# Rotary sum on another engine, output projection in token layout, first layer of a two-layer transformer on one core

## The reference

```python
q = jnp.einsum('bpd,hde->bphe', resid_pre, W_Q) + b_Q      # k, v alike
q = _apply_rotary(q, cos, sin)                             # k too: pairs (xr, xi) are turned
scores = jnp.einsum('bqhd,bkhd->bhqk', q, k) / ATTN_SCALE
scores = jnp.where(causal[None, None], scores, jnp.zeros((), dtype=scores.dtype))
max_v = jnp.max(jnp.abs(scores), axis=-1, keepdims=True)
sgn = jnp.sign(scores)
attn_w = sgn * jnp.exp(sgn * scores - max_v)
attn = attn_w / (jnp.sum(jnp.abs(attn_w), axis=-1, keepdims=True) + 1e-06)
z = jnp.einsum('bkhd,bhqk->bqhd', v, attn)
out = jnp.einsum('bqhd,hdm->bqm', z, W_O) + b_O
```

## Time and profile before

| | us |
|---|---|
| median of 3 runs | 992.29 (986.94 to 999.68) |
| the profiled execution, whole | 992.66 |
| its span between first and last instruction | 990.9 |
| first layer's heads, first to last `z_lo` | 54.4 to 452.3 |
| TensorE, VectorE, ScalarE, GpSimd busy | 866.4, 698.8, 508.4, 464.5 |

### The profile page before, as it was taken

How to read it: one execution, slowest core, us unless ns; L and a number is a source line. 1 busy time by engine, 2 the same in 40 slices (tenths; PEclk the granted TensorE clock), 3 DMA queues, 4 the chain that set the end, 5 groups by cost and what they waited for, 6 DMA issues and landing times.

```text
span 990.9 us, 14203 instructions
## 1 busy us (share of the span) xinstructions
PE 866.4 (87%) x3884; PEld 620.8 (63%) x3884; DVE 698.8 (71%) x1340; ACT 508.4 (51%) x1102; POOL 464.5 (47%) x393
## 2 busy tenths in 40 slices
PE   3799999999799999976799999578999997899997
PEld 2566666666566666654578887454444334678885
DVE  4789999989699999975755555856668814653344
ACT  2578887778578887853322222111546753222222
POOL 1646666656366666632256666422120002466663
PEclk9799999999899999997999999785789998999999
DMA  3222222222222222210033334053142100233332
GB/s 110 86 86 86 85 85 85 83 82 84 84 85 85 85 85 80 79 65 34 19 133 111 111 112 170 1 182 112 68 141 88 44 2 0 77 112 111 111 115 76
DMA packets 48270, 85.41 MB, mean 86 GB/s; under 512 B 7330, under 2 KB 18210, under 8 KB 48226
## 3 DMA queue, kind: packets, MB, share of 16 engines
q1 hardware_dynamic: 48226, 84.88, 25.3%
HBM read 58.38 MB, written 9.57 MB: 69 GB/s over the span
## 4 chain that ended last, share of the span: by engine, by line
PE 56%; DVE 18%; issue 8%; POOL 6%; ACT 6%; DMA 3%; DVEq 0%; SPq 0%; ACTq 0%; POOLq 0%
PE ps L719 16%; PE ps L731 7%; PE ps L315 5%; DVE ex L478 4%; PE ps L1236 3%; PE ps L1224 3%; DVE w L490 3%; DVE q_rot L451 3%; PE ps L366 3%; PE ps L1176 3%; PE ps L326 3%; PE ps L1155 3%; PE ps L358 2%; PE ps L348 2%; POOL q_sin L511 2%
## 5 line engine op out<-in xcount | busy, mean ns | idle before, releaser
L767 ACT ACTIVATE silu<-ps 128x512 f32<-128x512 f32 x68 | 40.7, 598 | 187.0 <-PE ps L719 187.0
L807 POOL TENSOR_TENSOR guw<-gu,cwb 128x512 f32<-128x512 f32 x64 | 96.6, 1511 | 82.9 <-DVE gu L854 65.5
L719 PE MATMUL ps<-xT_hi,ew_hi 128*128 128x512 f32 x272 | 107.6, 396 | 5.4 <-POOL ew_lo L797 5.4
L719 PE MATMUL ps<-xT_hi,ew_lo 128*128 128x512 f32 x272 | 106.2, 390 | 0.0
L719 PE MATMUL ps<-xT_lo,ew_hi 128*128 128x512 f32 x272 | 106.2, 390 | 0.0
L854 DVE TENSOR_TENSOR gu<-silu,ps 128x512 f32<-128x512 f32 x64 | 43.9, 687 | 87.7 <-PE ps L719 69.3
L797 POOL TENSOR_TENSOR ew_lo<-ew_raw,ew_hi 128x256 fp32r<-128x256 f32 (+1 forms) x68 | 80.1, 1179 | 54.4 <-DVE ew_hi L844 54.4
L1403 DVE TENSOR_REDUCE nm<-ps 128x1 f32<-128x512 f32 x128 | 81.1, 685 | 31.1 <-PE ps L1176 30.7
L451 DVE TENSOR_TENSOR q_rot<-q_cos,q_sin 128x512 f32<-128x512 f32 x64 | 86.4, 1388 | 11.5 <-POOL q_sin L511 10.1
L496 POOL TENSOR_TENSOR wqk_lo<-wqk_raw,wqk_hi 128x512 fp32r<-128x512 f32 x32 | 47.8, 1494 | 97.0 <-ACT wqk_hi L389 97.0
L490 DVE SCALAR_TENSOR_TENSOR w<-ex,rden,sgn 128x512 f32<-128x512 f32 (+3 forms) x128 | 90.7, 769 | 3.2
(11 more groups left out here) (172 smaller groups left out, 2128.5 us busy)
## 6 DMA issues: line engine op xcount, KB each, us to landing
q_sw<-q_in SPq DMA_DIRECT2D x128, 128.0 KB, 2.1
cwb<-cw_dram SPq DMA_DIRECT2D x30, 512.0 KB, 4.5
ew_raw<-in_ew SPq DMA_DIRECT2D x34, 384.0 KB, 3.0
wqk_raw<-in_wqk SPq DMA_DIRECT2D x32, 256.0 KB, 2.7
wv_raw<-in_wv SPq DMA_DIRECT2D x32, 128.0 KB, 2.3
wo_raw<-in_wo SPq DMA_DIRECT2D x32, 128.0 KB, 2.0
qs<-stk_q SPq DMA_DIRECT2D x16, 256.0 KB, 3.4
ks<-stk_k SPq DMA_DIRECT2D x16, 256.0 KB, 4.0
```

The lines of the kernel that those rows point to most:

```text
L719: last = pe.matmul(ps[:, 4 + 2 * h + u, :], ew[pw][:, p, col:col + P], half_of((xT_hi, xT_lo)[px][:, c, :], h), start=j == 0, stop=j == 3 ...
L807: pool.tensor_tensor(guw[:, h, :], gu[:, h, :], half_of(cwb[:, p, :], h), ALU.mult).then_inc(sem("guw"), 1)
```

## The change

The sum of the rotary halves moves from VectorE to GpSimd, and the sine products move there ahead of the causal masks. VectorE makes the cosine product from PSUM banks 5 and 6 with bias and cosine in one instruction, instead of from `q_in`; so TensorE now waits for `q_cos` and not for `q_ev` (the copy to `q_in`) before it writes these banks again, with the transposes and with the next projection. The output projection has `z` as its stationary and the weights as its moving operand, 12 matmuls of 256 columns instead of 6 of 512, so that the result lies in token layout as `x` does: no `aT`, no transposes back, no clearing (the first head of a batch starts the sum). The output bias of the layer, broadcast to all partitions, is added to `x` by GpSimd after steps 14 and 15. The loads of `wo`, `wv` and `wqk` have another order in SyncE's queue, and the constant rows for the second layer are written during the first experts instead of behind the last heads.

```diff
@@ a0_pe
                 for t in range(2):
+                    wait(pe, "q_cos", of_pair(n, t))
                     for j in range(3 * DC):
...
+                first = known(n) and n % H0 == 0
                 wait(pe, "z_lo", n + 1)
                 wait(pe, "wo_lo", n + 1)
-                for c in range(DC):
+                if first and n > 0:
+                    wait(pe, "x_add", 2)
+                for t in range(QT):
                     for j, (pw, pz) in enumerate(PARTS):
-                        last = pe.matmul(ps[:, c, :], wo[pw][:, c * P:(c + 1) * P], z0[pz][:, :],
-                                         start=False, stop=j == 2, skip_group_check=True)
+                        last = pe.matmul(ps[:, t // 2, t % 2 * D:(t % 2 + 1) * D], z0[pz][:, t * P:(t + 1) * P], wo[pw][:, :],
+                                         start=first and t % 2 == 0 and j == 0, stop=j == 2, skip_group_check=True)
...
                     if g:
-                        wait(pe, "q_ev", of_pair(min(n + 3, N0) if known(n) else n + 3, g - 1))
+                        wait(pe, "q_cos", of_pair(min(n + 3, N0) if known(n) else n + 3, g - 1))
@@ a0_act
                     wait(act, "q_ps", of_pair(n + 1, t))
-                    wait(act, "q_cos", of_pair(n, t))
                     wait(act, "q_sin", of_pair(n, t))
@@ a0_dve
-                    dve.tensor_tensor(q_cos[:, t, :], q_in[:, t, :], cos0[:, :], ALU.mult).then_inc(sem("q_cos"), 1)
+                    dve.scalar_tensor_tensor(out=q_cos[:, t, :], in0=ps[:, 5 + t, :], scalar=bqkv0[:, t, bass.ds(n, 1)],
+                                             in1=cos0[:, :], op0=ALU.add, op1=ALU.mult).then_inc(sem("q_cos"), 1)
...
-            if valid(i + 2, N0):
-                rotated(0)
-            if valid(i + 2, N0):
-                rotated(1)
@@ a0_pool
+                    wait(pool, "q_cos", of_pair(n + 1, t))
+                    wait(pool, "q_sin", of_pair(n + 1, t))
+                    wait(pool, "s", QT * (n - 1))
+                    pool.tensor_tensor(q_rot[:, par(2), t, :], q_cos[:, t, :], q_sin[:, t, :], ALU.add).then_inc(sem("q_rot"), 1)
@@ a0_sp
-            if valid(i + 1, N0):
-                n = i + 1
+            if valid(i, N0):
+                n = i
                 src = a["wo0"][head(n)]
                 wait(sp, "wo_lo", n)
                 sp.dma_start(wo_raw[:, :], src).then_inc(sem("wo_ld"), 16)
+            if valid(i + 2, N0):
+                n = i + 2
+                src = a["wv0"][head(n)]
+                wait(sp, "wv_lo", n)
+                sp.dma_start(wv_raw[:, :, :], src).then_inc(sem("wv_ld"), 16)
             if valid(i + 4, N0):
                 n = i + 4
                 src = a["wqk0"][head(n)]
                 wait(sp, "wqk_lo", n)
                 sp.dma_start(wqk_raw[:, :, :, :], src).then_inc(sem("wqk_ld"), 16)
...
+        def a0_at_pool(pool, i):
+            if i == H0 - 2:
+                pool.wait_ge(sem("bo0_ld"), 16)
+                pool.wait_ge(sem("xn"), NT)
+            if i in (H0 - 2, H0 - 1):
+                h = i - (H0 - 2)
+                pool.tensor_tensor(x[:, h * QT:(h + 1) * QT, :], x[:, h * QT:(h + 1) * QT, :],
+                                   bo0_b[:, :].unsqueeze(1).broadcast_to([P, QT, D]), ALU.add).then_inc(sem("x_bo0"), 1)
...
+            h = i // H0 - 1
+            dve.wait_ge(sem("x_bo0"), h + 1)
+            dve.wait_ge(sem("o"), i)
+            for k in range(2):
+                t = QT * h + 2 * k
+                dve.tensor_tensor(x[:, t:t + 2, :], x[:, t:t + 2, :],
+                                  ps[:, k, :].rearrange("p (t d) -> p t d", t=2), ALU.add).then_inc(sem("x_add"), 1)
+            if i == N0:
                 ln_stats(dve, 1, 0)
```

More of the change, by code:

```diff
@@ L184, in build_program @@
         cw_dram = [nc.dram_tensor(f"cw_dram{k}", (E, T), F32).ap() for k in range(2)]
-        bo_dram = nc.dram_tensor("bo_dram", (D,), F32).ap()
+        bo_dram = [nc.dram_tensor(f"bo_dram{k}", (D,), F32).ap() for k in range(2)]
         stk_dram = [nc.dram_tensor(f"stk_{t}", (N1 * P, S), F32).ap() for t in ("q", "k")]
@@ L445, in a0_dve @@
         def a0_dve(dve, i):
[L446 to L451, removed]
             if valid(i + 2, N0):
@@ L497, in a0_pool @@
                                    ALU.subtract).then_inc(sem("wqk_lo"), 1)
+            if valid(i + 2, N0):
+                n = i + 2
+                for t in range(2):
+                    wait(pool, f"swap{t}", 32 * (n + 1))
+                    wait(pool, "q_rot", of_pair(n, t))
+                    pool.tensor_tensor(q_sin[:, t, :], q_sw[:, t, :], sin0[:, :], ALU.mult).then_inc(sem("q_sin"), 1)
             if valid(i + 1, N0):
@@ L541, in a0_sp @@
                 sp.dma_start(wqk_raw[:, :, :, :], src).then_inc(sem("wqk_ld"), 16)
-            if valid(i + 3, N0):
-                n = i + 3
-                src = a["wv0"][head(n)]
-                wait(sp, "wv_lo", n)
-                sp.dma_start(wv_raw[:, :, :], src).then_inc(sem("wv_ld"), 16)
         batch = [0]
         odd = [0]
-        LOOPS0 = {1: (H0 - 6, 0), H0 + 1: (N0 - 6, 1)}
+        LOOPS0 = {3: (H0 - 6, 0), H0 + 3: (N0 - 6, 1)}
         def par(ahead):
@@ L567, in a0_steps @@
                     step(eng, i)
-                    if at and i in (H0, N0):
-                        at(eng, i // H0 - 1)
+                    if at:
+                        at(eng, i)
                     i += 1
-        def a0_between_sp(sp, b):
-            if b > 0:
-                return
-            ffn_sp(sp, 0)
-        def a1_early_sp(sp):
-            sp.wait_ge(sem("ones"), 1)
-            for t in range(2):
-                rows = stk_dram[t].rearrange("(b h r) s -> b h r s", b=B, r=STK)
-                for g in range(DC):
-                    for h in range(B):
-                        sp.dma_start(rows[h, g * H1 // 2:(g + 1) * H1 // 2, ROWS_S:STK, :],
-                                     fp(ones_r[:, :])).then_inc(sem("ones_st"), 16)
-            sp.dma_start(bo_dram.rearrange("(c p) -> c p", p=P), a["bo1"].rearrange("p c -> c p"), allow_slow_non_contiguous=True).then_inc(sem("bo_st"), 16)
@@ L587, in a0_zero_pe @@
-        def a0_zero_pe(pe, b):
-            if b == 0:
-                pe.wait_ge(sem("zero"), 1)
-            else:
-                pe.wait_ge(sem("x_add"), 2 * b)
-            for c in range(DC):
-                pe.matmul(ps[:, c, :], zero_r[:, 0:P], zero_r[:, :], start=True, stop=True, skip_group_check=True)
-        def a0_end_pe(pe, b):
-            back_pe(pe, "aT", 2 * b + 2, (0, 1), range(QT * b, QT * b + QT))
-            if b == 0:
-                a0_zero_pe(pe, 1)
-        def a0_end_act(act, b):
-            act.wait_ge(sem("o"), H0 * (b + 1))
-            for c in range(DC):
-                act.activation(aT[:, c, b * S:(b + 1) * S], ps[:, c, :], ACT.Identity,
-                               bias=bo0[:, c:c + 1]).then_inc(sem("aT"), 1)
@@ new lines, in ones_sp @@
+        def ones_sp(sp, t, g):
+            rows = stk_dram[t].rearrange("(b h r) s -> b h r s", b=B, r=STK)
+            sp.wait_ge(sem("ones"), 1)
+            for h in range(B):
+                sp.dma_start(rows[h, g * H1 // 2:(g + 1) * H1 // 2, ROWS_S:STK, :],
+                             fp(ones_r[:, :])).then_inc(sem("ones_st"), 16)
+        def a0_at_pool(pool, i):
[6 more added lines that the diff above has]
+                                   bo0_b[:, :].unsqueeze(1).broadcast_to([P, QT, D]), ALU.add).then_inc(sem("x_bo0"), 1)
@@ L611, in a0_end_dve, with a0_at_dve @@
+        def a0_at_dve(dve, i):
+            if i not in (H0, N0):
+                return
+            h = i // H0 - 1
+            dve.wait_ge(sem("x_bo0"), h + 1)
+            dve.wait_ge(sem("o"), i)
+            for k in range(2):
+                t = QT * h + 2 * k
+                dve.tensor_tensor(x[:, t:t + 2, :], x[:, t:t + 2, :],
+                                  ps[:, k, :].rearrange("p (t d) -> p t d", t=2), ALU.add).then_inc(sem("x_add"), 1)
+            if i == N0:
                 ln_stats(dve, 1, 0)
@@ L674, in step @@
                     load(m, p)
+                if f == 0 and known(m) and m in (2, 3, M - 3, M - 2):
+                    k = (2, 3, M - 3, M - 2).index(m)
+                    ones_sp(sp, k // 2, k % 2)
             ffn_steps(sp, step)
@@ L887, in ffn_dve @@
                 ln_xn(dve, 1, 0)
-                back_dve(dve, 2, (0, 1), range(QT, 2 * QT))
             else:
```

49 lines of the change are left out of this document (24 added, 25 removed).

## The result

The changed kernel takes 1083.55 us (median of 4 runs, 1081.76 to 1087.81) where the kernel before takes 993.52 us in the runs beside it: a ratio of 1.091, 95% interval 1.084 to 1.099. That is slower, by about 90 us; the prediction said 1105 us, with 1010 to 1135 as its range.

A forecast was written before the change was run, and what follows sets the result against it. Each first-layer head was taken as bound by a chain from transposes through VectorE's `w` to the next transposes. 992.7 + 76 (turns) + 42 (clock) - 2.5 (batch change) = 1108, stated as 1105 us, range 1010 to 1135.

The forecast's parts named there:

- Direction and mechanism: Whole kernel slower, as VectorE's `w` pieces and GpSimd operations take turns, three per head; slower beyond 2% had chance 0.80.
- Turns at `w`: First-layer heads: three GpSimd operations between the pieces of `w` instead of one, 15.3 us a head, +76 us over 28 heads.
- Cosine product from PSUM: First-layer heads: transposes wait for `q_cos`, +0.49 us a head; with -0.34 on the chain, +0.15 net.
- Rotary sum on GpSimd: First-layer heads: GpSimd's two added operations of about 1.25 us cost nothing while it has room; chain gains 0.34 us a head.
- TensorE's clock: First-layer heads: idle gaps of 3.4 us drop the granted clock to 0.50; 1.5 us a head, +42 us over 28.
- Layout: Output projection into token layout: twelve matmuls of 256 columns, 1.44 us against 1.4, so nothing.
- batch change: Between heads 16 and 17: copies, transposes and clearing go, bias additions come; net -2.5 us, between -9 and +3.
- The additions on GpSimd: Batch change: two output-bias steps of 2.37 us, each holding VectorE up once, 4.8 us.
- The end of the layer: End of the first layer: copies go, layer-norm sums stand behind the last projection; 0, between -2 and +3 us.
- the constant rows: Second layer's rows, moved into the experts' steps: cost at most their issue; 0, up to +4 us.
- the rotary part: First-layer heads: +76 us for turns, with the cosine product's part in it, and +42 us for the clock.
- the sign: Whole kernel: slower beyond 2% of 992 us, chance 0.80; within 0.08, faster 0.12.

The follow-up runs named there:

- e1: The changed kernel with GpSimd's sine product behind the causal masks again, ahead of the rotary sum: 1024.9 us, ratio 1.034.
- e2: The changed kernel with GpSimd's two sine products replaced by two memsets that read nothing from SBUF: 1018.9 us, ratio 1.031.
- e3: The changed kernel with the cosine product reading `q_in` again and the transposes waiting for ScalarE's eviction: 1075.0 us, ratio 1.084.
- e12: The kernel before with only the cosine product from PSUM, transposes and next projections waiting for it: 994.8 us, ratio 1.002.
- e11: The kernel before with masks ahead of `wqk_lo`, the changed load order, and the rotary sum on GpSimd behind the sine product: 1025.0 us, ratio 1.035.
- e7: The changed kernel with nine more useless matmuls of 512 columns per head in TensorE's gap before the transposes: 1066.7 us, ratio 1.073.
- e10: The kernel of e4 with the first layer's output bias left out, its stores, load and additions included: 996.5 us, ratio 1.007.
- e4: The kernel before with only the token-layout output projection, GpSimd's bias addition and no batch-change clearing; rotary steps and load order as before: 1015.9 us, ratio 1.028.
- e8: The kernel before with the whole rotary part and new load order; output projection, batch change and constants as before: 1066.9 us, ratio 1.075.

## Why the prediction was right, and where it was off

**Direction and mechanism** held. Step by step, with the profiled executions:

- *Turns at `w`.* Forecast: three pieces at 1.5 to 1.7 us, 15.3 us a head, +76 us. The pieces took 1.65, 1.35 and 1.48 us, the four together 4.99, and a head without a clock fall 14.78: +2.17 a head, 61 us over 28 heads (as in the forecast, the cosine product's part is in it). The mechanism was right; the term was some 15 us too large: `w` began where I had it, 9.8 us into the head, but its four pieces took 4.99 us where I had 5.5 (9.7 to 15.2). e1 and e2 show the cause: move the product, or let it read nothing, and the turns are gone. The trace agrees with the rule of the Trainium skill ("SBUF — State Buffer", "Who interferes with whom") that the prediction weighed: each of the three pieces was held anew. It agrees too with what the same section says of GpSimd instructions that only write: the memsets of e2 held nothing, `w` took 2.98 us there and 2.97 in e1.
- *Cosine product from PSUM.* Forecast +0.49 for the stall, +0.15 net. Measured 0.45 (e3) and 0.16 (e12). Right.
- *Rotary sum on GpSimd: nothing.* Right in this place: `q_rot` took 1.29 us a half and stood beside `nmax` and the wait for `z_hi`; heads take 12.77 us with the sum on GpSimd (e1) and 12.77 with it on VectorE (e12). e11 shows that this hung on the place: it is the same sum behind another queue, and `ex` is held.
- *TensorE's clock.* This step was mis-sized. I charged 1.5 us to each of 28 heads, +42 us. The clock fell in about every second head, for 3.4 us and not the 6.8 of the one row that I had the earlier trace rows, and cost 1.28 us there: 14 x 1.28 = 18 us; e7 gives 17. One row after one gap could not tell how often. The trace of before has a shorter fall as well, 3.3 us from 434.2 on behind a gap of 1.86 us, and I had not put it among the rows.
- *Layout: nothing; batch change: -2.5 us.* This failed. The part costs 17 us here and 26 alone. The additions on GpSimd cost 9.3 us by e10 and e4, not 4.8: I charged each its own length once, and did not follow what its delay lets later operations meet, nor the clock. The stores between two heads I had not priced at all, though the diff shows them: 12.8 us in e4, about 2 in the changed kernel. The end of the layer costs 2 us, inside its range. The first experts, where the constant rows are now written, take 159.9 us from their first to their last matmul in place of 154.9. That isn't shown to be the rows' price: the second experts, where nothing is written, take 155.8 in place of 151.8 (last section). I had put 0, up to 4, for the rows and nothing for the second experts.

By the two profiles: 61 + 18 in the heads, -2 for an earlier first head, and 2 each for the stores, the batch change (against heads of their own length) and the end of the layer make 83 us; the first experts add 5, the second 4, and the stage between them takes 3 less. That is 89, as the spans differ. The sum came within 2% because the rotary part was put 45 us too high (118 against 73) and the layout some 20 too low; the midpoint owes something to luck, the sign does not, for the rotary part alone (e8, 1066.9 us) is slower and inside the range. The layout's 17 us are not fully placed. By the profiles, whose spans differ by 13.5, the changed kernel takes 9 us more than e8 up to the last `z_lo`, 6 of them at the batch change, 2 at the end of the layer and 10 in the two stages of experts; against that stand 7 us less between the experts, where the code is the same. What makes the experts slower is open.

## What to carry to other kernels

Before work is moved from VectorE to GpSimd, or up in GpSimd's queue, ask which VectorE operations with both inputs in SBUF it will run beside: such a meeting can cost up to the whole of the other's operation. Here the place in the queue mattered more than the work moved: the sine product ahead of the masks cost 59 us, and the 2.7 us a head that VectorE shed gained nothing. `q_cos` (one input in PSUM, 1.40 us for two) and the reductions `nmax` (1.65 to 1.67 us for four, whichever GpSimd operation ran beside them) were not held. A stage that leaves TensorE a gap in every head pays twice, once for the gap and again for the clock. And of a moved step the small DMAs must be priced too: two stores of 1 KB in 4-byte pieces, ahead of transfers that a head waits for, held it for 12.8 us.
